# Normalised rows kept in DRAM as two fp16 halves, fp16 products in place of fp32 transposes, and gathers that leave empty places out

## The chip, the cores and the metric

The kernel runs on one core of a Trainium2 chip. The metric is the device time of the whole kernel in microseconds, the median of several executions. TensorE (PE in the profile, with its weight loads as PEld), VectorE (DVE), ScalarE (ACT), GpSimd (POOL) and SyncE (SP, which here only issues transfers) run side by side and meet at semaphores.

## The reference

One pre-norm block on 2 x 1024 tokens of width 512: attention with 32 heads (8 key and value heads of width 16), then a mixture of experts. Only the second half matters here:

```python
flat = x.reshape(b * t, d)                      # 2048 x 512, layer-normalised
logits = flat @ router_w                        # 64 experts
scores = jax.nn.softmax(logits, axis=-1)
_, topk_idx = jax.lax.top_k(logits + router_bias, K)   # K = 4
...
g = jax.nn.silu(jnp.einsum('nd,edf->nef', flat, wg))   # F = 128
u = jnp.einsum('nd,edf->nef', flat, wu)
routed = jnp.einsum('ne,nef,efd->nd', comb, g * u, wd)
...
shared = jnp.einsum('nsh,shd->nd', sg * su, swd)       # 2 shared experts of 512
return (routed + shared).reshape(b, t, d)
```

Each token goes to 4 of 64 experts, so there are 8192 (token, expert) places to compute. With the inputs given, the experts get from 13 to 432 tokens each.

## The kernel before

The attention part is untouched. After it come these stages.

**Normalisation and router.** Tokens stand in 16 tiles of 128, in four groups. TensorE runs, group by group: four output projections (`project`), then for the group before, four transposes of normalised rows (`turn_tokens`, fp32, into PSUM banks 4 and 5 by turns), then their router products (`logits`). `xn2` is a ring of four fp32 tiles of normalised rows, written by VectorE. ScalarE copies each turned tile out of PSUM twice (L900, L901); a bank is free for the next turn only after L901. SyncE stores each normalised tile to `xn2_rows` in DRAM, and after every fourth store issues the load of the next shared weights (`load_stage`). GpSimd is idle until it scales the last shared weights (`swd_scale`, L751).

**Shared experts, routing.** `shared_up` products for the first two groups of 512 tokens. For the first twelve of its 16 chunks `hidden` (L781) is on GpSimd, and TensorE's chunk n waits for `hidden` of chunk n - 2. VectorE works the routing out: places are ordered by expert and cut in tiles of 64, an expert's last tile being partly empty; 192 tiles are laid on 8 lanes of 24 rounds. The table `tab_t` holds for each place its token; an empty place holds 0, so it gathers token 0.

**Routed experts.** 96 pairs of lanes, four to a round, in a loop written out for one round. For pair n GpSimd copies the 128 token numbers (L799) and gathers rows (L801) to the ring `xg` of four tiles. TensorE runs in fixed order: `turn_slots` of pair n + 1 (four fp32 transposes of `xg`, read at every fourth column, L1280), `expert_up` of n (L1293), `turn_hidden` of n - 1 (L1301), `expert_down` of n - 2 (L1309). ScalarE copies the turned rows (L941), VectorE the results (L1668), and ScalarE issues the stores to `slot_y`. SyncE loads an expert's weights to a lane when the lane's expert changes: the up weights of pair n for the next round wait for `e_up` of n in this one, so they have three pairs' time to land. A lane whose expert stays, or that has none, skips its load.

**The rest.** The shared experts of the last two groups of tokens, while GpSimd gathers the rows of `slot_y` and VectorE adds them by gate (`mix`).

In the reference's inputs the 64 experts fill 161 of the 192 tiles; the 12,288 places hold 8192 tokens. Tiles are laid lane by lane, so lane 7 has none, lane 6 none from round 17 on. Counting from the reference's routing, rounds 17, 18 and 19 hold 207, 240 and 189 tokens in 512 places each.

Of the kernel before, what the change touches and what calls it, by code (L numbers as in the profile page):

```python
# [12 lines left out]
P = 128  # L13
# [146 lines left out]
def build_block(nc, x, wq, wk, wv, wo, router_w, router_bias, wgu, wd, swg, swu, swd, out):  # L160
    ctx = ExitStack()
    with ctx:
# [3 lines left out]
        def sem(name):  # L166
            return ctx.enter_context(nc.semaphore(name))
# [25 lines left out]
        k_stacks = nc.dram_tensor("k_stacks", [KVH, 3, HD, NTOK], F16)  # L193
        xn2_rows = nc.dram_tensor("xn2_rows", [NTOK, D], FP32)
        slot_y = nc.dram_tensor("slot_y", [SLOTS, D], FP32)
# [10 lines left out]
        small = sb("small", [P, 1536])  # L206
        ident = sb("ident", [P, P])
        eps_s = sb("eps_s", [P, 1])
        warm = sb("warm", [P, 1])
# [27 lines left out]
        def q_part(u, h, part):  # L237
# [27 lines left out]
        xn2, = carve_all(w_att, 0, ([P, 4, D], FP32))  # L265

        shared_w, swd_w, tmp, mask = carve_all(
            att, 0, ([P, 4, 2 * C * D], F16), ([P, 2, HC * D], F16), ([P, NT, E], FP32),
# [13 lines left out]
        def hidden(n):  # L282
# [10 lines left out]
        lane_w += [carve(flat_xt, n * 3 * C * F, [P, 3, C * F])[0] for n in range(4)]  # L293
        xg, xgt, yb, sg, ht, hg = carve_all(w_att, 0, ([P, 4, D], FP32), ([P, 2, D], FP32), ([P, 2, D], FP32),
                                            ([P, 2, P], FP32), ([P, 2, P], FP32), ([P, 2, P], FP32))
# [22 lines left out]
        ident_zero = sem("ident_zero")  # L318
        ident_set = sem("ident_set")
        mask_zero = sem("mask_zero")  # L320
        mask_steps = sem("mask_steps")
# [50 lines left out]
        xn2_ready = sem("xn2_ready")  # L372
        xn2_stored = sem("xn2_stored")
        turn2_done = sem("turn2_done")
# [86 lines left out]
        def _(sp):  # L461
# [84 lines left out]
            for t in range(NT):  # L546
                sp.wait_ge(xn2_ready, t + 1)
                sp.dma_start(xn2_rows[t * P:(t + 1) * P, :], xn2[:, t % 4, :]).then_inc(xn2_stored, 16)
                if t % 4 == 3:
                    load_stage(2 + t // 4)  # L550
# [50 lines left out]
        def _(pool):  # L601
# [15 lines left out]

            part_scale(0)
            for b in range(BATCH):
                pool.memset(v_head[b][:, :, :], 1 / X_SCALE).then_inc(v_ones, 1)  # L620
# [107 lines left out]
            for l in range(2):  # L728
# [8 lines left out]
                .then_inc(consts, 1)  # L737
            pool.tensor_copy(token_f[:, :], token_f[:, :].bitcast(U32)).then_inc(consts, 1)
            pool.tensor_copy(iota_t[:, :, :], iota_t[:, :, :].bitcast(U32)).then_inc(consts, 1)
            pool.wait_ge(consts, 15)  # L740

            pool.affine_select(out=tile_no[:, LANES:], in_=tile_no[:, LANES:], compare_op=ALU.is_gt, fill=-1.0, base=0,
                               pattern=[[0, LANES]], channel_multiplier=1).then_inc(consts, 1)

            def swd_half(n):
# [49 lines left out]
            def gather_tokens(i, j):  # L795
                n = JP * i + j

                wait(pool, xg_turned, n - 3)
                pool.tensor_copy(idx[:, j:j + 1], tab_t[:, bass.ds(j * LANE_TILES + i, 1)]).then_inc(idx_set, 1)  # L799
                wait_alone(pool, idx_set, n + 1, pool_passed)  # L800
                pool.indirect_dma_start(out=xg[:, j, :], out_offset=None, in_=xn2_rows[:, :],  # L801
                                        in_offset=bass.IndirectOffsetOnAxis(ap=idx[:, j:j + 1], axis=0))\
                    .then_inc(xg_in[j], 16)

            pool.wait_ge(table_ready, 1)
            pool.wait_ge(xn2_stored, 16 * NT)
            for j in range(JP):
# [16 lines left out]
        def _(act):  # L824
# [58 lines left out]
            exps(KVH - 1)  # L883

            for g in range(4):
                act.wait_ge(ln2_aggr, g + 1)
                act.activation(std[:, 4 * g:4 * g + 4], mv[:, 4 * g:4 * g + 4, 1], ACT.Sqrt, bias=eps_s[:, :])\
                   .then_inc(ln2_std, 1)
                act.wait_ge(stage_in[g % 2], 16 * (g // 2 + 1))
                act.activation(shared_w[:, 2 * (g // 2), (g % 2) * C:(g % 2 + 1) * C, :],  # L890
                               w_stage[:, g % 2, :].rearrange("p (c n) -> p c n", c=C), ACT.Copy, scale=W_SCALE)\
                   .then_inc(w_hi_ready, 1)
                for t in range(4 * g, 4 * g + 4):
                    act.wait_ge(turn2_done, t + 1)
                    if t >= 4:

                        act.wait_ge(logits_done, t - 3)
                        act.wait_ge(x_lo_ready, t - 3)
                    src = bank(4 + t % 2).rearrange("p (c t) -> p c t", c=C)
                    act.activation(x_turned[:, t % 4, :, :], src, ACT.Copy).then_inc(xt2_ready, 1)  # L900
                    act.activation(x_hi[:, :, t * P:(t + 1) * P], src, ACT.Copy, scale=X_SCALE).then_inc(x_hi_ready, 1)  # L901
            def swd_high(n):
                act.wait_ge(swd_scaled, n + 1)
                part = slice(n % 2 * C // 2, (n % 2 + 1) * C // 2)
                act.activation(swd_w[:, 0, n * C // 2:(n + 1) * C // 2, :],
                               w_stage[:, n // 2, :].rearrange("p (c n) -> p c n", c=C)[:, part, :], ACT.Copy)\
                   .then_inc(swd_hi_ready, 1)
# [72 lines left out]
        def _(pe):  # L980
# [293 lines left out]
            def turn_slots(n, k, i):  # L1274
                j = k % JP
                pe.wait_ge(xg_in[j], 16 * (i + k // JP + 1))

                wait(pe, xgt_ready, n - 1)
                for c in range(C):
                    mm = pe.transpose(PS[:, (k % 2) * BANK + c * P:(k % 2) * BANK + (c + 1) * P],  # L1280
                                      xg[:, j, c:D:C], ident[:, :])
                mm.then_inc(xg_turned, 1)
# [42 lines left out]

            pe.wait_ge(table_ready, 1)
            turn_slots(0, 0, 0)
            expert_pairs(0, True, False)
# [13 lines left out]
        def _(dve):  # L1342
# [143 lines left out]
            for g in range(4):  # L1486
# [16 lines left out]
                if g:  # L1503

                    dve.wait_ge(xn2_stored, 64 * g)
                    dve.wait_ge(turn2_done, 4 * g)
# [126 lines left out]

            dve.wait_ge(xn2_stored, 16 * NT)
            for k in range(TOPK):
                hot_rows(k)

            for g in range(EARLY):
                for n in range(ON_POOL, HC * (g + 1)) if g else ():
                    shared_hidden(n)  # L1640
                    if n > ON_POOL:
                        hidden_low(n - 1)
                    if n == TABLE_AT + 1:
                        dve.wait_ge(table_done, 1)
                        dve.tensor_copy(tab_t[:, :], bank(6, PAIRS)).then_inc(table_ready, 1)
                if g:
                    hidden_low(HC * (g + 1) - 1)
                for t in range(4 * g, 4 * g + 4) if g else ():
                    shared_add(t)
# [97 lines left out]
```

## Time and profile before

| what | value |
|---|---|
| median of 3 runs | 1257.54 us (1248.75 to 1260.25) |
| the profiled execution | 1258.9 us, its span 1257.2 us |
| mean granted TensorE clock | 0.973 of full speed |
| TensorE busy | 90% of the span |
| VectorE, ScalarE, GpSimd busy | 59%, 40%, 34% |
| HBM read, written | 225.08 MB, 41.42 MB |

Times in the trace are microseconds from the start of the span. The chain of waits is read backwards from the last instruction: each row is what the next one waited for. A matmul's row includes the time until its result is out, so successive starts, not durations, give the pace of TensorE.

### The profile page before, as it was taken

The numbers are of one execution on the slowest core, as the hardware profiler recorded it, in microseconds if no ns is written. First come the engines' busy times: TensorE is split into PE (matmuls) and PEld (weight loads), VectorE is DVE, ScalarE is ACT, GpSimd is POOL, SyncE is SP. The second block draws the span as 40 slices with busy tenths as digits, with TensorE's granted clock in tenths as the row PEclk, the third lists the DMA queues.
The fourth block names the chain that finished last, engine by engine and source line by source line (L and its number), as shares of the span: only waits on it lengthen the run. The fifth ranks groups of instructions, "written<-read, shape, count | busy, mean of one in ns | idle before, by whom it ended". The sixth has DMA issues, their size and how long they took to land.

```text
span 1257.2 us, 27761 instructions
## 1 busy us (share of the span) xinstructions
PE 1136.3 (90%) x9096; PEld 518.4 (41%) x9097; DVE 745.4 (59%) x1198; ACT 501.2 (40%) x944; POOL 423.0 (34%) x548
## 2 busy tenths in 40 slices
PE   6967889988988998998998989999999989997998
PEld 3523233333333332355443445545554444443443
DVE  6746899998999985675798113322333222336373
ACT  3211777887887878434412112222222212211010
POOL 5300233333233333202828322222322222236560
PEclk9978899999999999999999999999999999998999
DMA  8243311221232120242000368878887789656552
GB/s 235 70 132 98 70 45 40 60 55 38 39 74 39 38 51 8 94 142 101 1 1 0 118 210 286 266 251 289 285 266 223 241 281 308 224 132 202 160 168 66
DMA packets 75766, 169.98 MB, mean 135 GB/s; under 512 B 13764, under 2 KB 16324, under 8 KB 75716
## 3 DMA queue, kind: packets, MB, share of 16 engines
q1 hardware_dynamic: 45972, 100.59, 26.6%
q0 software_dynamic: 12800, 41.95, 11.6%
q10 hardware_dynamic: 16944, 26.75, 6.2%
q8 instruction: 34, 0.56, 0.2%
q14 instruction: 16, 0.13, 0.0%
HBM read 225.08 MB, written 41.42 MB: 212 GB/s over the span
## 4 chain that ended last, share of the span: by engine, by line
PE 59%; DVE 18%; issue 9%; DMA 7%; ACT 3%; POOL 1%; SPq 1%; another core or an unknown queue 1%; DVEq 0%; ACTq 0%; POOLq 0%
PE PS L1293 13%; PE PS L1184 9%; PE PS L1309 7%; DVE maxes L1365 7%; PE PS L1101 5%; PE PS L1266 5%; DVE max_low L1367 5%; PE PS L1280 4%; PE PS L989 4%; PE PS L1154 3%; DMA ring<-in_L_ffn_wg_dram 3%; PE PS L1050 2%; PE PS L1079 2%; PE PS L1301 2%; DMA q_stacks<-att 1%
## 5 line engine op out<-in xcount | busy, mean ns | idle before, releaser
L877 ACT ACTIVATE att<-PS 128x512 f32<-128x512 f32 x576 | 312.5, 594 | 93.6 <-PE PS L1079 88.0
L1365 DVE TENSOR_REDUCE maxes<-PS 128x2 f32<-128x128 f32 (+7 forms) x256 | 186.6, 748 | 33.3 <-PE PS L994 33.1
L1184 PE MATMUL PS<-XN,att 128*128 128x512 f16 x768 | 174.6, 389 | 15.6 <-issue 7.7
L1101 PE MATMUL PS<-att,v_head 128*32 128x256 f32 (+1 forms) x2560 | 180.4, 373 | 0.9 <-POOL att L692 0.9
L989 PE MATMUL PS<-att 48*128 48x512 f16 (+7 forms) x768 | 128.3, 332 | 51.1 <-DVE max_low L1367 24.3
L1367 DVE TENSOR_REDUCE max_low<-PS 128x2 f32<-128x1024 f32 x128 | 154.9, 1210 | 11.5 <-PE PS L989 11.0
L1668 DVE COPY w_att<-PS 128x512 f32<-128x512 f32 x96 | 66.4, 692 | 104.1 <-DMA slot_y<-w_att 77.2
L1656 DVE TENSOR_TENSOR w_att<-w_att,PS 128x128 f32<-128x128 f32 x96 | 27.6, 288 | 168.4 <-issue 97.9
L941 ACT ACTIVATE w_att<-PS 128x512 f32<-128x512 f32 x96 | 57.2, 597 | 172.5 <-PE PS L1280 171.6
L692 POOL TENSOR_SCALAR_AFFINE_SELECT att<-att 128x512 f32<-128x512 f32 (+1 forms) x96 | 75.1, 789 | 142.8 <-ACT att L877 141.7
L1184 PEld LDWEIGHTS PS<-XN,att 128*128 128x128 f16 x768 | 76.0, 100 | 112.2 <-issue 19.2
L801 POOL DMA_INDIRECT w_att<-xn_rows,idx x96 | 93.7, 976 | 75.6 <-POOL idx L799 73.2
L1079 PE MATMUL PS<-att 50*128 50x512 f16 (+1 forms) x640 | 113.1, 366 | 5.0 <-ACT att L877 2.6
L989 PEld LDWEIGHTS PS<-att 48*128 48x128 f16 x768 | 37.2, 93 | 185.1 <-DVE maxes L1365 79.9
L1293 PE MATMUL PS<-ring,w_att 128*64 128x256 f32 x768 | 95.0, 390 | 10.5 <-DMA ring<-in_L_ffn_wg_dram 9.4
L1293 PE MATMUL PS<-XT,w_att 128*64 128x256 f32 x768 | 94.6, 389 | 3.3 <-issue 3.3
L919 ACT ACTIVATE w_att<-PS 128x512 f32<-128x512 f32 x32 | 19.1, 597 | 186.5 <-PE PS L1184 136.8
L819 POOL DMA_INDIRECT ring<-slot_y,small x64 | 69.5, 1087 | 68.5 <-DMA slot_y<-w_att 27.5
L1266 PE MATMUL PS<-att,XT 128*128 128x512 f16 x384 | 84.1, 379 | 4.6 <-DVE XT L1621 2.2
L799 POOL COPY idx<-small 128x1 uint32 (+1 forms) x96 | 18.0, 188 | 208.5 <-PE PS L1280 193.5
L1101 PEld LDWEIGHTS PS<-att,v_head 128*32 128x32 f32 x2560 | 56.4, 109 | 72.2 <-issue 45.6
L1280 PEld LDWEIGHTS PS<-ident,w_att 128*128 128x128 f32 x384 | 53.6, 209 | 75.3 <-issue 74.4
(169 smaller groups left out, 1380.2 us busy)
## 6 DMA issues: line engine op xcount, KB each, us to landing
ring<-in_L_ffn_wg_dram SPq DMA_DIRECT2D x96, 512.0 KB
XT<-in_L_ffn_wg_dram SPq DMA_DIRECT2D x96, 512.0 KB
ring<-in_L_ffn_wd_dram SPq DMA_DIRECT2D x96, 256.0 KB
XT<-in_L_ffn_wd_dram SPq DMA_DIRECT2D x96, 256.0 KB
slot_y<-w_att ACTq DMA_DIRECT2D x192, 128.0 KB
att<-q_stacks SPq DMA_DIRECT2D x64, 192.0 KB, 3.8
q_stacks<-att SPq DMA_DIRECT2D x24, 256.0 KB
att<-k_stacks SPq DMA_DIRECT2D x64, 96.0 KB, 3.9
```

The source lines that it names most:

```text
L801: pool.indirect_dma_start(out=xg[:, j, :], out_offset=None, in_=xn2_rows[:, :], in_offset=bass.IndirectOffsetOnAxis(ap=idx[:, j:j + 1], ax ...
L877: act.activation(probs[:, n0 % RING, u * BANK:(u + 1) * BANK], bank((2 * n0 + u) % EXP_BANKS), ACT.Exp, scale=HD ** -0.5 / QK_SCALE ** 2). ...
L989: mm = pe.matmul(bank(at + u, n), q_max[b][rows, t * P:(t + 1) * P], k_max[b][rows, lo:lo + n], start=True, stop=not diagonal)
L1079: mm = pe.matmul(PS[:, at:at + 2 * qn], k_exp[b][rows, kt * P:(kt + 1) * P], q_exp[b][rows, 2 * q0:2 * (q0 + qn)] .rearrange("p (t h q) -> ...
L1101: mm = pe.matmul(PS[32 * r:32 * r + 32, at:at + qn], v_head[b][:, kt, :], probs[:, (NS * b + s) % RING, a:a + qn], start=s in (0, NS0), st ...
L1184: mm = pe.matmul(bank(2 * (n % 2) + k), shared_w[:, 2 * k + w, C * s + c, at:at + P], v[:, c, tokens], start=(c == 0 and w == 0 and v is x ...
L1266: mm = pe.matmul(bank(4 + t % 2), v[:, hc, (t % 4) * P:(t % 4 + 1) * P], swd_w[:, w, hc, :], start=(hc == 0 and w == 0 and v is hidden_hi) ...
L1280: mm = pe.transpose(PS[:, (k % 2) * BANK + c * P:(k % 2) * BANK + (c + 1) * P], xg[:, j, c:D:C], ident[:, :])
L1293: mm = pe.matmul(PS[l * SUB:(l + 1) * SUB, at:at + 2 * F], xgt[:, j % 2, c * P + l * SUB:c * P + (l + 1) * SUB], lane_w[2 * j + l][:, 0:2, ...
L1309: mm = pe.matmul(PS[l * SUB:(l + 1) * SUB, (4 + j % 2) * BANK:(5 + j % 2) * BANK], hg[:, j % 2, l * SUB:(l + 1) * SUB], lane_w[2 * j + l][ ...
L1365: dve.reduce_max(maxes[b][:, :, t], src, AXX).then_inc(side_read, 1)
L1367: dve.reduce_max(max_low[:, :, t - LOW_TILES], src, AXX).then_inc(side_read, 1)
```

## The change

`xn2_rows` gets rows of 1024 fp16 numbers: the high half (the value rounded to fp16, written by ScalarE, `row_high`) and the low half (the rest, by GpSimd, `row_low`), both with the columns reordered so that the four chunks of 128 are contiguous. A row is still 2 KB. `turn_slots` then multiplies both halves by a fp16 identity and sums in PSUM: eight fp16 products instead of four fp32 transposes. Empty places of the table hold 2048 instead of 0, and the gather leaves a number above 2047 out; `xg` is zeroed once first.

```diff
+        row_parts, = carve_all(att, 8192, ([P, 4, 2 * D], F16))
...
             for t in range(NT):
-                sp.wait_ge(xn2_ready, t + 1)
-                sp.dma_start(xn2_rows[t * P:(t + 1) * P, :], xn2[:, t % 4, :]).then_inc(xn2_stored, 16)
+                sp.wait_ge(row_lo_done, t + 1)
+                sp.dma_start(xn2_rows[t * P:(t + 1) * P, :], row_parts[:, t % 4, :])\
+                    .then_inc(xn2_stored[t % 4], 16)
...
+            pool.wait_ge(ident_set, 1)
+            pool.tensor_copy(ident_h[:, :], ident[:, :]).then_inc(ident_h_set, 1)
...
+            def row_low(t):
+                pool.wait_ge(row_hi_done, t + 1)
+                hi, lo = [row_parts[:, t % 4, k * D:(k + 1) * D].rearrange("p (c k) -> p c k", c=C) for k in range(2)]
+                pool.tensor_tensor(lo, xn2[:, t % 4, :].rearrange("p (k c) -> p c k", c=C), hi, ALU.subtract)\
+                    .then_inc(row_lo_done, 1)
+
+            for t in range(NT):
+                row_low(t)
...
                 pool.indirect_dma_start(out=xg[:, j, :], out_offset=None, in_=xn2_rows[:, :],
-                                        in_offset=bass.IndirectOffsetOnAxis(ap=idx[:, j:j + 1], axis=0))\
+                                        in_offset=bass.IndirectOffsetOnAxis(ap=idx[:, j:j + 1], axis=0),
+                                        bounds_check=NTOK - 1, oob_is_err=False)\
                     .then_inc(xg_in[j], 16)
...
+            pool.memset(xg[:, :, :].rearrange("p n d -> p (n d)"), 0.0).then_inc(xg_zero, 1)
+            pool.wait_ge(xg_zero, 1)
...
+            def row_high(g):
+
+                for t in range(4 * g, 4 * g + 4):
+                    act.wait_ge(xn2_ready, t + 1)
+                    if t >= 4:
+                        act.wait_ge(xn2_stored[t % 4], 16 * (t // 4))
+                    act.activation(row_parts[:, t % 4, 0:D].rearrange("p (c k) -> p c k", c=C),
+                                   xn2[:, t % 4, :].rearrange("p (k c) -> p c k", c=C), ACT.Copy).then_inc(row_hi_done, 1)
...
                         act.wait_ge(logits_done, t - 3)
                         act.wait_ge(x_lo_ready, t - 3)
+                    if t % 4 == 0:
+                        row_high(g)
...
                 for c in range(C):
-                    mm = pe.transpose(PS[:, (k % 2) * BANK + c * P:(k % 2) * BANK + (c + 1) * P],
-                                      xg[:, j, c:D:C], ident[:, :])
+                    for part in range(2):
+                        mm = pe.matmul(PS[:, (k % 2) * BANK + c * P:(k % 2) * BANK + (c + 1) * P],
+                                       xg[:, j, part * D + c * P:part * D + (c + 1) * P], ident_h[:, :],
+                                       start=part == 0, stop=part == 1)
...
-                    dve.wait_ge(xn2_stored, 64 * g)
+                    dve.wait_ge(row_lo_done, 4 * g)
                     dve.wait_ge(turn2_done, 4 * g)
...
-                        dve.tensor_copy(tab_t[:, :], bank(6, PAIRS)).then_inc(table_ready, 1)
+                        dve.tensor_scalar(tab_t[:, :], bank(6, PAIRS), float(NTOK), None, ALU.add).then_inc(table_ready, 1)
```

`token_f` holds the token less 2048, which the last line of the diff adds back. `row_parts` lies where the down weights of the shared experts come later, so ScalarE's first `swd_high` waits for all stores.

The order of instructions moves in three places. On ScalarE in the last group of the normalisation stage (PS is PSUM, w_att holds `xn2`, ring the turned fp32 tiles, XN the fp16 ones, att in L915 `row_parts`), before:

```order
L887 ACTIVATE std<-mv,eps_s 128x4 [waits ln2_aggr]
L890 ACTIVATE att<-ring 128x2048 [waits stage_in1]
L900 ACTIVATE ring<-PS 128x512 [waits x_lo_ready,logits_done,turn2_done]
L901 ACTIVATE XN<-PS 128x4x128
...
L919 ACT_TABLE_LOAD
L919 ACTIVATE w_att<-PS 128x512 [waits up_done]
```

and now:

```order
L920 ACTIVATE std<-mv,eps_s 128x4 [waits ln2_aggr]
L923 ACTIVATE att<-ring 128x2048 [waits stage_in1]
L915 ACTIVATE att<-w_att 128x512 [waits xn2_ready,x_lo_ready,xn2_stored0,logits_done,turn2_done]
L915 ACTIVATE att<-w_att 128x512 [waits xn2_stored1,xn2_ready]
L915 ACTIVATE att<-w_att 128x512 [waits xn2_stored2,xn2_ready]
L915 ACTIVATE att<-w_att 128x512 [waits xn2_stored3,xn2_ready]
L935 ACTIVATE ring<-PS 128x512
L936 ACTIVATE XN<-PS 128x4x128
```

The four row copies stand behind the wait for the group's first turn and ahead of the copies that free its banks; so it is in all four groups. On GpSimd, from the last constant of the routing to the first two hidden chunks of the shared experts (ring holds the staged weights), before:

```order
L742 AFFINE_SELECT small<-small 128x8 [waits consts]
L751 TENSOR_SCALAR ring<-ring 128x1024 [waits stage_in0] x2
L781 TENSOR_TENSOR w_att<-w_att 128x512 [waits up_copied,silu_done] x2
L761 TENSOR_TENSOR XT<-w_att,XT 128x512 [waits hidden_hi_done]
L751 TENSOR_SCALAR ring<-ring 128x1024 [waits stage_in1]
```

and now:

```order
L753 AFFINE_SELECT small<-small 128x8 [waits consts]
L759 TENSOR_TENSOR att<-w_att,att 128x512 [waits row_hi_done] x16
L771 TENSOR_SCALAR ring<-ring 128x1024 [waits stage_in0] x2
L801 TENSOR_TENSOR w_att<-w_att 128x512 [waits up_copied,silu_done] x2
L781 TENSOR_TENSOR XT<-w_att,XT 128x512 [waits hidden_hi_done]
```

All sixteen subtractions stand ahead of the scaling of the shared weights, and that ahead of the hidden chunks. On TensorE, one pair of the routed experts in the loop, before:

```order
L1280 MATMUL PS<-ident,w_att 128x128 x4
L1288 REGISTER_ALU
L1293 MATMUL PS<-XT,w_att 64x256 x8
L1301 MATMUL PS<-ident,w_att 128x128
L1309 MATMUL PS<-ring,w_att 64x512 x2
```

and now:

```order
L1319 MATMUL PS<-ident_h,w_att 128x128 x8
L1328 REGISTER_ALU
L1333 MATMUL PS<-XT,w_att 64x256 x8
L1341 MATMUL PS<-ident,w_att 128x128
L1349 MATMUL PS<-ring,w_att 64x512 x2
```

Nothing changes place there; the first row has eight products for four.

## Rows read from the trace of the kernel before

**Rows 1.** The page, busy time by engine, whole span.
```profile
PE 1136.3 (90%) x9096; PEld 518.4 (41%) x9097; DVE 745.4 (59%) x1198; ACT 501.2 (40%) x944; POOL 423.0 (34%) x548
```
**Rows 2.** Stretches: busy time by engine, clock, DMA share and GB/s.
```profile
531.00:596.00 65.00, 59.49 (x363) 37.75 (x361) 43.77 (x76) 26.33 (x44) 6.09 (x3) 1.00 0.37 130
728.00:1115.00 387.00, 371.21 (x2405) 189.94 (x2402) 113.55 (x289) 83.88 (x192) 106.46 (x184) 0.99 0.78 258
```
**Rows 3.** The chain of waits, 580 to 625 us: start, us, what.
```profile
588.86 0.05 ACT ring L900
...
595.43 1.27 POOL w_att L781
...
596.84 22.32 PE PS L1184 x96
```
**Rows 4.** Instructions in order of time, ScalarE, third group's turns.
```profile
571.67 0.60 ACT L900 ACTIVATE ring<-PS 128x512 f32<-128x512 f32 x1 [11.20 <-PE PS L1163]
572.17 0.59 ACT L901 ACTIVATE XN<-PS 128x512 f16<-128x512 f32 x1
```
**Rows 5.** Instructions in order of time, VectorE and GpSimd, 570 to 608 us.
```profile
589.98 0.69 DVE L1480 SCALAR_TENSOR_TENSOR XN<-ring,XN 128x512 f16<-128x512 f32 x1 [7.34 <-ACT XN L901]
...
604.72 3.44 DVE L1545 TENSOR_TENSOR XT<-small 128x1024 bf16<-128x1024 f32 x2
...
570.69 5.52 POOL L751 TENSOR_SCALAR ring<-ring 128x1024 f32<-128x1024 f32 x2 [48.56 <-DMA ring<-in_L_ffn_swd_dram]
...
599.48 1.16 POOL L761 TENSOR_TENSOR XT<-w_att,XT 128x512 f16<-128x512 f32 x1 [1.56 <-ACT XT L911]
...
604.88 2.19 POOL L781 TENSOR_TENSOR w_att<-w_att 128x512 f32<-128x512 f32 x1 [1.51 <-ACT w_att L923]
```
**Rows 6.** Two lines' weight loads: min/median/max ns, first and last start.
```profile
L1163 PEld LDWEIGHTS PS<-ident,w_att x64: 138/140/143, 536.4 to 591.3; 128*128 128x128 f32 x64
...
L1280 PEld LDWEIGHTS PS<-ident,w_att x384: 195/211/220, 728.5 to 1104.2; 128*128 128x128 f32 x192
```
**Rows 7.** Instructions in order of time, TensorE, one pair.
```profile
898.85 0.75 PE L1280 MATMUL PS<-ident,w_att 128*128 128x128 f32 x4
...
902.67 0.75 PE L1280 MATMUL PS<-ident,w_att 128*128 128x128 f32 x4
903.35 1.95 PE L1293 MATMUL PS<-ring,w_att 128*64 128x256 f32 x16
```
**Rows 8.** Instructions in order of time, TensorE, value projections (L1060).
```profile
32.93 2.84 PE L1060 MATMUL PS<-att,XT 128*128 128x128 f16 x48 [0.18 <-POOL att L616]
35.60 5.34 PE L1050 MATMUL PS<-XT,att 128*128 128x512 f16 x24
...
105.71 0.83 PE L1060 MATMUL PS<-att,XT 128*128 128x128 f16 x12
106.48 0.39 PE L989 MATMUL PS<-att 48*128 48x512 f16 x2
```
**Rows 9.** The chain of waits, routed experts: start, us, what.
```profile
742.56 3.15 PE PS L1293 x16
...
1006.74 9.36 DMA ring<-in_L_ffn_wg_dram
...
1042.69 7.93 DMA ring<-in_L_ffn_wg_dram
...
1107.73 1.73 PE PS L1293 x16
```
**Rows 10.** A stretch around one stall, columns as in rows 2.
```profile
1000.00:1020.00 20.00, 16.28 (x100) 8.32 (x96) 4.74 (x13) 3.22 (x7) 4.63 (x8) 0.91 0.88 302
```
**Rows 11.** GpSimd in order of time, then L801 and L645 by line.
```profile
904.56 0.97 POOL L801 DMA_INDIRECT w_att<-xn_rows,idx  x1 [0.79 <-POOL idx L799]
...
L801 POOL DMA_INDIRECT w_att<-xn_rows,idx x96: 970/974/1182, 711.9 to 1090.4; - x96
...
L645 POOL MEMSET att<- x2: 948/948/949, 32.7 to 33.6; 128x1024 f16 x2
```

More of the change, by code:

```diff
@@ L193, in build_block @@
         k_stacks = nc.dram_tensor("k_stacks", [KVH, 3, HD, NTOK], F16)
-        xn2_rows = nc.dram_tensor("xn2_rows", [NTOK, D], FP32)
+        xn2_rows = nc.dram_tensor("xn2_rows", [NTOK, 2 * D], F16)
         slot_y = nc.dram_tensor("slot_y", [SLOTS, D], FP32)
@@ L207, in build_block @@
         ident = sb("ident", [P, P])
+        ident_h = sb("ident_h", [P, P], F16)
         eps_s = sb("eps_s", [P, 1])
@@ L293, in build_block @@
         lane_w += [carve(flat_xt, n * 3 * C * F, [P, 3, C * F])[0] for n in range(4)]
-        xg, xgt, yb, sg, ht, hg = carve_all(w_att, 0, ([P, 4, D], FP32), ([P, 2, D], FP32), ([P, 2, D], FP32),
+        xg, xgt, yb, sg, ht, hg = carve_all(w_att, 0, ([P, 4, 2 * D], F16), ([P, 2, D], FP32), ([P, 2, D], FP32),
                                             ([P, 2, P], FP32), ([P, 2, P], FP32), ([P, 2, P], FP32))
@@ L319, in build_block @@
         ident_set = sem("ident_set")
+        ident_h_set = sem("ident_h_set")
+        row_hi_done = sem("row_hi_done")
+        row_lo_done = sem("row_lo_done")
+        xg_zero = sem("xg_zero")
         mask_zero = sem("mask_zero")
@@ L372, in build_block @@
         xn2_ready = sem("xn2_ready")
-        xn2_stored = sem("xn2_stored")
+        xn2_stored = [sem(f"xn2_stored{n}") for n in range(4)]
         turn2_done = sem("turn2_done")
@@ L737, in _ @@
                 .then_inc(consts, 1)
-            pool.tensor_copy(token_f[:, :], token_f[:, :].bitcast(U32)).then_inc(consts, 1)
+            pool.tensor_scalar(token_f[:, :], token_f[:, :].bitcast(U32), float(-NTOK), None, ALU.add)\
+                .then_inc(consts, 1)
             pool.tensor_copy(iota_t[:, :, :], iota_t[:, :, :].bitcast(U32)).then_inc(consts, 1)
@@ L801, in gather_tokens @@
                 pool.indirect_dma_start(out=xg[:, j, :], out_offset=None, in_=xn2_rows[:, :],
-                                        in_offset=bass.IndirectOffsetOnAxis(ap=idx[:, j:j + 1], axis=0))\
+                                        in_offset=bass.IndirectOffsetOnAxis(ap=idx[:, j:j + 1], axis=0),
+                                        bounds_check=NTOK - 1, oob_is_err=False)\
                     .then_inc(xg_in[j], 16)
             pool.wait_ge(table_ready, 1)
-            pool.wait_ge(xn2_stored, 16 * NT)
+            for n in range(4):
+                pool.wait_ge(xn2_stored[n], 16 * (NT // 4))
+            pool.memset(xg[:, :, :].rearrange("p n d -> p (n d)"), 0.0).then_inc(xg_zero, 1)
+            pool.wait_ge(xg_zero, 1)
             for j in range(JP):
@@ L903, in swd_high @@
                 act.wait_ge(swd_scaled, n + 1)
+                if n == 0:
+                    for m in range(4):
+                        act.wait_ge(xn2_stored[m], 16 * (NT // 4))
                 part = slice(n % 2 * C // 2, (n % 2 + 1) * C // 2)
@@ L1326, in _ @@
             pe.wait_ge(table_ready, 1)
+            pe.wait_ge(ident_h_set, 1)
             turn_slots(0, 0, 0)
@@ L1632, in hot_rows @@
                    .then_inc(tile_hot, 1)
-            dve.wait_ge(xn2_stored, 16 * NT)
+            for n in range(4):
+                dve.wait_ge(xn2_stored[n], 16 * (NT // 4))
             for k in range(TOPK):
```

## The prediction

> **What bounds the kernel now.** I read the busy table first: TensorE 90% [rows 1], so the question is always what moves TensorE. The stretches then give the two stages that the change touches [rows 2]: normalisation and router, 59.5 us of TensorE work in 65 us, and the routed experts, 371.2 in 387, both at full clock. In neither is another engine near its limit; the transfers are at 0.78 in the second. Third, the timeline of one pair of routed experts [rows 7]: turns start at 898.85 and 902.67, so a pair takes 3.82 us, and TensorE's work fills it. Fourth, the chain. In the experts it runs on TensorE and leaves it only where a lane's new weights are late: at 1006.74 a weight transfer holds it for 9.36 us, at 1042.69 another for 7.93 [rows 9]. How much that is in all: from `expert_up` of pair 3 (742.56) to that of pair 95 (1107.73) there are 365.2 us; 92 pairs at 3.825 would be 351.9; 13.3 us are stalls, 3.7 of them in the 20 us around the first of these transfers, where TensorE was busy for 16.28 [rows 10]. Between the stages the chain passes from TensorE to ScalarE at 588.86 (the last group's turned tiles), to GpSimd at 595.43 (`hidden` of chunk 0), and back at 596.84, after which TensorE has work for 22 us without leaving the chain [rows 3]. So in the first stage ScalarE's copies and GpSimd's first chunk are on the path, though both engines are mostly idle.
>
> **The change, part by part**, against the profiled execution (1258.9; the median of the runs is 1.4 lower).
>
> *Row copies on ScalarE, on the path.* In each group TensorE turns two tiles, then waits for ScalarE's L901 to free a bank; ScalarE sat idle 11.2 us before that and starts as soon as the turn is there [rows 4]. Four copies of 128x512 now stand between. Successive copies start 0.50 us apart (571.67, 572.17), so a group gets 1.96 to 2.0 us longer and nothing hides it: the projections behind are in TensorE's order. Four groups: **+7.8 us**. The copies read `xn2` at a step of 16 bytes. The nearest row on such a read is TensorE's own: weight loads of the contiguous `xn2` take 140 ns, of `xg` at the same step 211 [rows 6], half as much again. By that ScalarE's would be 0.73 us, +11.7. I take 7.8, since the 0.50 is ScalarE's own row and the 211 another engine's, and keep 11.7 as the upper end. The lower end is 7: I see no cover for less.
>
> *Row subtractions on GpSimd.* In the first three groups four of them take some 5 us beside ScalarE's copies. VectorE, which now waits for them, waits for the same group's turns anyway, and what it writes then, like the stores and the `load_stage` behind them on SyncE, is wanted a group later, 17.2 us (571.67 to 588.86, [rows 3, 4]): nothing. In the last group, ScalarE starts its copies at 588.86 + 3 x 1.96 = 594.7, GpSimd its first subtraction at 595.3. A like operation (L761, two inputs, fp16 out) takes 1.16 us alone [rows 5]; four end at 600.0. VectorE's four L1480 (0.69 each) fall in there, and GpSimd operations that meet VectorE's with two inputs get longer (L781 from 1.27 to 2.19 beside L1545): I add 1.5, so 601.5. Behind them stand two `swd_scale`, which before had been done at 570.69, where GpSimd was idle (5.52 for two, so 607.0), then `hidden` of chunk 0 (1.27 and 0.14 to TensorE): 608.4, where it was 596.84. That is 11.6 in all, 3.8 beyond ScalarE's 7.8. If the 16-byte step costs GpSimd the half that it costs the weight loads, four times 0.58 come on top: 6.1. Between these I take the middle, **+5.0**; ends 3 and 9. Late next would be the routing's `ranks` on TensorE; VectorE is delayed only by ScalarE's part and has slack against TensorE there, so the whole delay is passed on. `load_stage` of the last weights is issued only after the last subtraction, near 603, and is wanted by the third `swd_scale` near 611; 1 MB at the 302 GB/s of [rows 10] is 3.5 us, an estimate, so it is in time.
>
> On the lock behind these longer operations the Trainium skill (SBUF — State Buffer, "SBUF: two separate sides") says that a VectorE operation with two SBUF inputs and a GpSimd one that reads SBUF exclude each other for a whole instruction. The 2.19 agrees. By that rule all four L1480 would be waited for in full, 2.8 instead of my 1.5, and the sum would be 1.3 higher.
>
> *Small things.* The fp16 identity is one GpSimd copy while it waits for weights; `token_f` and `tab_t` are exchanged one for one. Zeroing `xg` (4096 fp16) is four times L645's 0.95 = 3.8 us; the first gather was issued at 711.9 and the first turn came at 728.5 [rows 6, 11], so 17 us of shared experts cover it; without that cover it would cost 3.8. **0.**
>
> *Turning the slots.* Before, 0.68 us from the first turn to the first `expert_up` [rows 7]. The value projections are the same products (128x128 fp16 weights, 128 columns): 48 in 2.67 us, 0.0556 each; and twelve of them before another kind took 0.77, which is 12 x 0.0556 and 0.10 for the changeover [rows 8]. Eight then take 0.445 + 0.10 = 0.545, a gain of 0.135 a pair, over 95 pairs **-12.8 us**. Ends: with no changeover 0.235 (-22); with a second changeover 0.035 (-3).
>
> *Gathers.* 4096 of 12,288 places are empty: 8.4 MB less. That is worth only what it takes off the stalls. In the stretch around the largest one the core moved 302 GB/s at a share of 0.88 [rows 10]; a round's four gathers are 1.05 MB in 15.3 us. In rounds 17 to 19 between 47% and 37% of the places are filled, so some 0.6 MB go, 2.1 us at that rate. At the two late transfers of [rows 9] I take 2.1 each, at the other places, with fuller rounds, 1.5 in all. Against it, weights have three pairs' time to land, and that gets 3 x 0.135 = 0.4 shorter, at five stalls 2.0. Together -3.7, of which I take **-3.0**; ends +2 (no relief) and -9.
>
> *Sum.* 7.8 + 5.0 - 12.8 - 3.0 = **-3.0**: 1255.9 by the profiled execution, 1254.5 by the median; I say **1255**. A measurement of this kernel can tell a difference of about 1% (12.6 us) from none.
>
> **The rivals.**
>
> *A. The strided reads cost more (ends slower than before).* ScalarE at 0.73: copies of the last group start at 597.5, the first subtraction at 598.3; four at 1.74 and 1.5 of meetings end at 606.8; `swd_scale` 612.3; TensorE resumes at 613.7, 16.9 us late. With the rule of whole operations and longer `swd_scale` beside VectorE's search, 20. Gains stay 15.8. +1 to +4: **1261**. It decides when the first stage's delay passes 15.8 us. For it: the 211 against 140 ns. Against: no row shows ScalarE or GpSimd slowed by a step.
> The Trainium skill (GPSIMD Engine Reference, "Performance pitfalls for Q7 kernels") prices SBUF reads at steps above 8 bytes at half as much again. It would make GpSimd's part 6.1 rather than 3.8. No row here shows GpSimd at such a step.
>
> *B. GpSimd's gather becomes the bound.* A gather with a limit may take longer to issue. Gap and gather are 0.79 + 0.97 = 1.76 us of a pair's 3.69 [rows 11], with the short copy of the numbers under 2. It decides from a gather of 2.7 us; at 2.9, 95 pairs would lose 0.2 each: +19 - 3, **1273**. Nothing speaks for it.
>
> *C. Everything gained.* The changeover is hidden, -22, and the stalls mostly go, -9; the cost is 12.8: -18, **1239**. For it: the weight stalls lie where the gathers are emptiest.
>
> *D. Leaving out doesn't relieve.* Skipped places cost the queues what they cost before, or the stalls are a matter of when the weights are issued: +2 instead of -3: **1260**.
>
> **How the numbers follow.** Forecast 0.50 (1250 to 1260), A 0.17, B 0.06, C 0.15, D 0.12. All but B and C lie within 1%. Taking the bounds at both ends, the range is **1240 to 1269**. Faster by over 1% is C and a little of the forecast's lower side, 0.19; slower is B and the upper end of A, 0.12; within 1%, 0.69.
>
> **What would show it.** ScalarE: sixteen copies of 0.6 us, four before each group's first L900's like, and groups of 19.1 us instead of 17.2. GpSimd: subtractions of 1.2 us or, if A, 1.7; TensorE's gap before its third shared chunk 10 to 13 us longer in place. A pair at 3.69 us in place of 3.825. Stalls from pair 3 to 95 near 10 us. If TensorE's pair is not shorter, the turning term is wrong; if the stage ahead of the experts is longer by over 16 us, A.

## The result: 1.3% slower, where the forecast was 0.2% faster

| | before | changed |
|---|---|---|
| median | 1258.34 us (4 runs) | 1274.53 us (4 runs) |
| ratio, 95% interval | 1 | 1.0127 (1.0091 to 1.0163) |
| span of the profiled execution | 1257.2 us | 1271.0 us |
| mean granted TensorE clock | 0.973 | 0.958 |

One execution of a later run, the repeated early copies, took 2635.21 us, for a reason that is not known, and is left out of that run's median and ratio.

The chain of waits of the changed kernel, at the first `expert_up`, at that of pair 3 and at the last one (start, us, what):

```profile
762.09 1.95 PE PS L1333 x16
...
772.83 1.95 PE PS L1333 x16
...
1117.47 1.73 PE PS L1333 x16
```

The first `expert_up` starts at 762.09, 31.9 us later than before (730.17); from it to the last one there are 355.4 us instead of 377.6; the end is 13.8 us later. So the stage ahead lost 32, the experts gave 22.2 back, and 4.1 went in the tail, which no part of the change touches. The experts' gain is larger than forecast (15.8). The loss ahead of them is two and a half times the 12.8 that were forecast, and all of it lies in the normalisation stage. The stretches say what kind of loss it is (columns as in [rows 2]; 531 to 630 answers to the first of them, the next two are in it):

```profile
531.00:630.00 99.00, 79.45 (x355) 54.07 (x352) 42.90 (x72) 43.11 (x60) 29.27 (x19) 0.75 0.25 85
...
541.00:549.00 8.00, 8.00 (x40) 7.75 (x38) 4.92 (x10) 4.50 (x7) 1.02 (x1) 0.50 0.59 199
...
555.00:561.00 6.00, 6.00 (x29) 2.71 (x28) 1.38 (x2) 0.00 (x0) 0.00 (x0) 1.00 0.00 0
```

TensorE's work, nearly the same instructions, is 79.5 us instead of 59.5, at a granted clock of 0.75; inside a group the clock is 0.50, which is its level of 1.2 GHz, and back at 1.00 some 14 us later. TensorE and ScalarE in order of time show where it falls, in the first group:

```profile
534.75 1.04 PE L1201 MATMUL PS<-ident,w_att 128*128 128x128 f32 x8
540.64 2.05 PE L1201 MATMUL PS<-ident,w_att 128*128 128x128 f32 x8 [4.86 <-ACT XN L936]
542.49 6.93 PE L1209 MATMUL PS<-router_s,ring 128*128 128x64 f32 x32
549.21 12.17 PE L1192 MATMUL PS<-att,XT 128*128 128x512 f16 x48
561.22 1.04 PE L1201 MATMUL PS<-ident,w_att 128*128 128x128 f32 x8
```
```profile
535.38 4.15 ACT L915 ACTIVATE att<-w_att 128x512 f16<-128x512 f32 x4 [5.05 <-PE PS L1201]
...
588.74 4.15 ACT L915 ACTIVATE att<-w_att 128x512 f16<-128x512 f32 x4 [16.47 <-PE PS L1201]
```

ScalarE's four copies take 4.15 us, 1.03 each. TensorE sits idle for 4.86 us after two turns, and after that everything is slow: eight turns in 2.05 us, 32 router products in 6.93 (before: 3.68), and part of the projections. A group is 26.5 us (534.75 to 561.22; the next two take 26.9 and 27.1), where ScalarE's turned copies were 17.2 us apart [rows 3, 4].

One pair of routed experts in the changed kernel, which answers to [rows 7]:

```profile
902.99 0.62 PE L1319 MATMUL PS<-ident_h,w_att 128*128 128x128 f16 x8
903.54 1.95 PE L1333 MATMUL PS<-XT,w_att 128*64 128x256 f32 x16
905.41 0.33 PE L1341 MATMUL PS<-ident,w_att 128*128 128x128 f32 x1
905.67 1.08 PE L1349 MATMUL PS<-ring,w_att 128*64 128x512 f32 x4
906.69 0.62 PE L1319 MATMUL PS<-ident_h,w_att 128*128 128x128 f16 x8
```

The turn takes 0.55 us (902.99 to 903.54), a pair 3.70. From pair 3 (772.83) to pair 95 there are 344.6 us; 92 pairs at 3.70 are 340.4, so 4.2 us of stalls are left of 13.3.

### The profile page after: what moved, and what is told of

Its sections match the earlier page's. It is cut to its first block, busy times and chain, and to the rows that moved or that the text cites. A ratio compares the mean times of both kernels' runs of the same rounds, so it can differ in the third digit from the quotient of the medians.

```text
span 1271.0 us, 28676 instructions
## 1 busy us (share of the span) xinstructions
PE 1142.1 (90%) x9480; PEld 523.4 (41%) x9481; DVE 750.1 (59%) x1198; ACT 517.5 (41%) x960; POOL 453.7 (36%) x566
## 4 chain that ended last, share of the span: by engine, by line
PE 64%; DVE 17%; issue 8%; DMA 4%; ACT 3%; POOL 1%; SPq 1%; DVEq 0%; ACTq 0%; POOLq 0%
PE PS L1333 14%; PE PS L1222 10%; PE PS L1349 7%; DVE maxes L1406 7%; PE PS L1304 6%; PE PS L1139 5%; DVE max_low L1408 4%; PE PS L1319 4%; PE PS L1027 4%; PE PS L1192 4%; PE PS L1088 2%; PE PS L1117 2%; PE PS L1341 2%; PE PS L1209 2%; DMA q_stacks<-att 1%
## 5 line engine op out<-in xcount | busy, mean ns | idle before, releaser
L1222 PE MATMUL PS<-XN,att 128*128 128x512 f16 x768 | 178.3, 394 | 16.0 <-issue 7.8
L1408 DVE TENSOR_REDUCE max_low<-PS 128x2 f32<-128x1024 f32 x128 | 154.8, 1210 | 11.9 <-PE PS L1027 11.7
L821 POOL DMA_INDIRECT w_att<-xn_rows,idx x96 | 99.1, 1032 | 81.8 <-POOL idx L819 78.3
L1222 PEld LDWEIGHTS PS<-XN,att 128*128 128x128 f16 x768 | 76.6, 101 | 115.8 <-issue 22.7
L984 ACT ACTIVATE w_att<-PS 128x128 f32<-128x128 f32 x96 | 26.6, 277 | 132.3 <-PE PS L1333 102.5
L1319 PEld LDWEIGHTS PS<-ident_h,w_att 128*128 128x128 f16 x768 | 43.3, 98 | 75.3 <-issue 75.0
```

What stands on the lines that cost most here:

```text
L1222: mm = pe.matmul(bank(2 * (n % 2) + k), shared_w[:, 2 * k + w, C * s + c, at:at + P], v[:, c, tokens], start=(c == 0 and w == 0 and v is x ...
L1319: mm = pe.matmul(PS[:, (k % 2) * BANK + c * P:(k % 2) * BANK + (c + 1) * P], xg[:, j, part * D + c * P:part * D + (c + 1) * P], ident_h[:, :],
L1408: dve.reduce_max(max_low[:, :, t - LOW_TILES], src, AXX).then_inc(side_read, 1)
```

## The experiments

All ratios are against the kernel before, run beside on the same chip, with the 95% interval.

**Theory 1**: ScalarE's copies, where they stand, open a gap on TensorE in each group, and TensorE comes back from it at half clock; the clock costs more than the gap. **Theory 2**: the stage is slow because of the added work itself, GpSimd's subtractions and the loads behind them, or reads beside TensorE's.

### The copies early

```diff
             for g in range(4):
                 ...
+                row_high(g)
                 for t in range(4 * g, 4 * g + 4):
                     act.wait_ge(turn2_done, t + 1)
                     ...
-                    if t % 4 == 0:
-                        row_high(g)
```

Expected:

> The changed kernel with one edit: ScalarE's four row copies of a group stand ahead of its wait for the group's first turn, where ScalarE is idle for 11 us (5 us in the first group), instead of behind it. Theory 1 (the copies open a gap of 4.9 us on TensorE in each group, and TensorE comes back from it at half clock): both go, the normalisation stage takes 65 us again instead of 99, granted clock 1.00 there, the kernel 1258 - 22 = 1236 us (1231 to 1242). Theory 2 (the stage is slower because GpSimd's sixteen subtractions and the later load of the shared down weights stand in the way, or because ScalarE's and GpSimd's reads disturb TensorE's): the work is the same, the stage stays above 85 us, the kernel above 1258.

Measured: 1233.99 us against 1251.83, ratio 0.9846 (0.9803 to 0.9888); once more on another chip:

> The kernel with the early copies once more, on the same chip as the spread places, for a comparison free of the chip. It should repeat its ratio of 0.985 (0.981 to 0.989), with 4 to 6 us of stalls.

Measured: 1239.13 against 1259.94, ratio 0.9835 (0.9796 to 0.9873); the stalls from pair 3 on are 4.1 us in the first of these runs and 5.4 in the second. From the first run, the stretch that answers to the first of [rows 2], TensorE's gap and GpSimd:

```profile
531.00:596.00 65.00, 60.27 (x362) 37.40 (x360) 45.46 (x82) 41.32 (x57) 39.87 (x18) 1.00 0.37 130
```
```profile
558.05 0.63 PE L1200 MATMUL PS<-ident,w_att 128*128 128x128 f32 x4 [0.83 <-ACT XN L935]
559.03 0.63 PE L1200 MATMUL PS<-ident,w_att 128*128 128x128 f32 x4 [0.35 <-ACT XN L935]
559.50 3.68 PE L1208 MATMUL PS<-router_s,ring 128*128 128x64 f32 x32
```
```profile
581.10 9.15 POOL L759 TENSOR_TENSOR att<-w_att,att 128x512 f16<-128x512 f32 x4 [7.99 <-ACT att L915]
590.23 5.51 POOL L771 TENSOR_SCALAR ring<-ring 128x1024 f32<-128x1024 f32 x2
597.77 2.49 POOL L801 TENSOR_TENSOR w_att<-w_att 128x512 f32<-128x512 f32 x2 [2.04 <-ACT w_att L960]
```

The same copies and subtractions cost nothing here: clock 1.00, gap 0.83 us, a group 17.2. The last group's four subtractions even take 9.15 us, where those of the changed kernel take 5.4 to 5.9 a group (the first of them stand beside VectorE's L1520 and L1554, 580.28 to 584.98), and are still done before GpSimd is wanted. Theory 2 falls. This version beats both kernels.

### TensorE kept busy through the gap

```diff
             def turn_tokens(t):
                 ...
+                if t % 4 == 1:
+                    for n in range(20):
+                        pe.matmul(bank(4 + t % 2), wo_hi[:, n % C, 0:P], wo_lo[:, n % C, :], start=True, stop=True)
                 for c in range(C):
                     mm = pe.transpose(...)
```

and, in the second run, 40 transposes of the tile to the same bank in their place:

```diff
+                    for n in range(40):
+                        pe.transpose(PS[:, (4 + t % 2) * BANK + n % C * P:(4 + t % 2) * BANK + (n % C + 1) * P],
+                                     xn2[:, t % 4, n % C * P:(n % C + 1) * P], ident[:, :])
```

Expected:

> The changed kernel, and TensorE computes 20 fp16 products of 512 columns (some 4.3 us) into the free bank between the first and the second turn of each group; their result is written over. They add work and take no wait away. Theory 1: TensorE is busy through ScalarE's copies, the clock stays at 1.00 from the second group on, router products take 3.7 us a group instead of 6.9 and the projections behind them 10.5 instead of 12.2, a group 22 us instead of 26.9: the kernel 1253 to 1258 us, 17 to 21 below the changed one. Theory 2 (the products are slow for another reason, reads beside ScalarE's): no gain, 1274 or some us more.

> As the run with filling products, but the filler is 40 more fp32 transposes of the group's second tile (some 4.5 us at 0.11 us each), written over as well. If transposes keep the clock up as products do: 1253 to 1259 us, clock 1.00 in the stage. If a transpose counts as no work for the clock: the clock falls as in the changed kernel, each transpose takes twice as long, 1274 to 1285 us.

Measured: 1250.28 and 1250.41 against 1251.83, ratios 0.9993 (0.9967 to 1.0018) and 0.9983 (0.9951 to 1.0014). Added work makes the changed kernel 1.3% faster. With the filling transposes:

```profile
560.13 0.60 PE L1205 MATMUL PS<-ident,w_att 128*128 128x128 f32 x4
560.57 4.53 PE L1202 MATMUL PS<-ident,w_att 128*128 128x128 f32 x40
564.93 0.60 PE L1205 MATMUL PS<-ident,w_att 128*128 128x128 f32 x4
566.21 0.63 PE L1205 MATMUL PS<-ident,w_att 128*128 128x128 f32 x4 [0.68 <-ACT XN L936]
```

and with the filling products:

```profile
558.58 0.63 PE L1204 MATMUL PS<-ident,w_att 128*128 128x128 f32 x4 [0.62 <-ACT XN L936]
559.55 0.63 PE L1204 MATMUL PS<-ident,w_att 128*128 128x128 f32 x4 [0.34 <-ACT XN L936]
560.02 3.68 PE L1212 MATMUL PS<-router_s,ring 128*128 128x64 f32 x32
```

ScalarE holds the banks as long as in the changed kernel, but router products are at 3.68 us. A group takes 21.3 to 21.4 us. So the wait for the banks costs about 4.1 us a group, and the clock 5 to 6 more. Here GpSimd does come into the way: with TensorE at full pace it waits 4.03 us for the first hidden chunk, 2.4 more than before (1.62), which is the term forecast at 5.0; in the changed kernel TensorE was so late that 0.36 was left of it.

The Trainium skill (TensorE: Matmul & The Clock Gate, "Part 4: PE-mode transpose") says that a transpose doesn't count as work for the clock as a product does. Here the measurement differs: with 40 fp32 transposes in the gap (4.53 us) the granted clock stayed at 1.00 behind it in all four groups, as with 20 fp16 products (4.48 us).

### The step of the read

```diff
-    act.activation(row_parts[:, t % 4, 0:D].rearrange("p (c k) -> p c k", c=C),
-                   xn2[:, t % 4, :].rearrange("p (k c) -> p c k", c=C), ACT.Copy).then_inc(row_hi_done, 1)
+    act.activation(row_parts[:, t % 4, 0:D], xn2[:, t % 4, :], ACT.Copy).then_inc(row_hi_done, 1)
...
-    xg[:, j, part * D + c * P:part * D + (c + 1) * P]
+    xg[:, j, part * D + c:(part + 1) * D:C]
```

and the subtraction likewise. Expected:

> The changed kernel, but the halves keep the columns in their order: ScalarE and GpSimd read the fp32 rows contiguously, and TensorE reads the gathered halves at every fourth column instead (a step of 8 bytes). If the step of 16 bytes is what doubles ScalarE's copy: 0.50 us each instead of 1.03, the gap on TensorE 2.7 us instead of 4.9, GpSimd 1.16 instead of 1.36. By theory 1 the shorter gap costs at least 2.1 us less a group, 1266 at most; if it is also short enough for the clock to hold, 1250 or less (a group 19.2 us). Weight loads of the slots at a step of 8 bytes may take longer than 98 ns; if the pace of a pair stays 3.70 us they are hidden.

Measured: 1257.84 against 1251.83, ratio 1.0058 (1.0022 to 1.0094). In order of time, ScalarE, then TensorE:

```profile
558.39 2.19 ACT L915 ACTIVATE att<-w_att 128x512 f16<-128x512 f32 x4 [15.45 <-PE PS L1200]
```
```profile
561.70 0.72 PE L1200 MATMUL PS<-ident,w_att 128*128 128x128 f32 x4 [2.90 <-ACT XN L935]
562.67 1.08 PE L1200 MATMUL PS<-ident,w_att 128*128 128x128 f32 x4 [0.26 <-ACT XN L935]
563.55 6.92 PE L1208 MATMUL PS<-router_s,ring 128*128 128x64 f32 x32
```
```profile
559.10 4.50 POOL L759 TENSOR_TENSOR att<-w_att,att 128x512 f16<-128x512 f32 x4 [19.40 <-ACT att L915]
```

The step of 16 bytes is what doubled ScalarE's copies: 2.19 us for four at a step of 4 bytes, 4.15 at 16. GpSimd's four subtractions take 4.50 us instead of 5.4. And without the step the clock falls too, after a gap of 2.90 us: this is exactly the 2 us a group that the prediction had priced, and router products behind it still run at half clock. Read at a step of 8 bytes the slots' weight loads take 113 ns instead of 98; a pair takes 3.72 us for 3.70, so nearly all of that is hidden.

### How long a gap

To see this away from the change, the kernel before got two idle copies on ScalarE:

```diff
                 for t in range(4 * g, 4 * g + 4):
                     act.wait_ge(turn2_done, t + 1)
+                    if t % 4 == 0:
+                        for n in range(2):
+                            act.activation(spare[:, n, :], xn2[:, 0, :], ACT.Copy)
```

Expected:

> The kernel before, with two more copies of 128x512 on ScalarE (contiguous, to a spare place, read by nobody) ahead of each group's turned copies. They lengthen TensorE's gap in each group from 0.83 to 1.8 us and do nothing else. Known: a gap of 0.83 us leaves the clock at 1.00, one of 2.9 us (plain columns) brings the slow stretch. If the clock also falls after 1.8 us: a group 22 us or more instead of 17.2, the kernel 18 us or more slower, ratio 1.014 or more. If it holds: a group 18.2 us, 4 us slower, ratio 1.003.

Measured: 1271.83 against 1260.73, ratio 1.0107 (1.005 to 1.0163), between the two expectations:

```profile
536.75 0.63 PE L1167 MATMUL PS<-ident,w_att 128*128 128x128 f32 x4 [1.86 <-ACT XN L905]
537.73 0.63 PE L1167 MATMUL PS<-ident,w_att 128*128 128x128 f32 x4 [0.35 <-ACT XN L905]
538.19 6.68 PE L1175 MATMUL PS<-router_s,ring 128*128 128x64 f32 x32
...
559.93 0.63 PE L1167 MATMUL PS<-ident,w_att 128*128 128x128 f32 x4 [1.86 <-ACT XN L905]
560.90 0.63 PE L1167 MATMUL PS<-ident,w_att 128*128 128x128 f32 x4 [0.35 <-ACT XN L905]
561.37 3.68 PE L1175 MATMUL PS<-router_s,ring 128*128 128x64 f32 x32
```

The same gap of 1.86 us was followed by the low clock in the first group and not in the second; the third and the fourth had it again. One microsecond of waiting more costs 1 us in one group (18.2 us, 557.03 to 575.25) and 6 in another (23.2 us, 533.85 to 557.03).

The length of the gap doesn't decide it alone. The kernel before has the low clock too, where its stage ends (TensorE alone; columns: stretch, us, busy, clock, DMA share, GB/s) and behind the stall of [rows 10]:

```profile
596.00:600.00 4.00, 3.16 (x8) 0.57 0.00 0
600.00:604.00 4.00, 4.00 (x20) 1.00 0.00 0
...
1016.00:1020.00 4.00, 3.58 (x17) 0.57 1.04 413
1020.00:1024.00 4.00, 4.00 (x28) 1.00 0.88 290
```

The first comes after a wait of 1.62 us (for GpSimd's chunk 0), the second after one of 3.72. In the changed kernel, against that, a wait of 2.93 us left the clock at 1.00:

```profile
721.48 4.71 PE L1222 MATMUL PS<-XN,att 128*128 128x512 f16 x21 [2.93 <-POOL w_att L801]
```
```profile
718.00:722.00 4.00, 1.07 (x6) 1.00 0.00 0
722.00:726.00 4.00, 4.00 (x20) 1.00 0.02 4
```

Behind the gaps inside the groups the clock stayed low for 10 to 14 us, behind these two for some 4. What makes the difference was not tried.

### What leaving places out is worth

Two runs take the other half of the change apart: the early copies with every place gathered again,

```diff
-            pool.tensor_scalar(token_f[:, :], token_f[:, :].bitcast(U32), float(-NTOK), None, ALU.add)\
+            pool.tensor_copy(token_f[:, :], token_f[:, :].bitcast(U32))\
                 .then_inc(consts, 1)
...
-                                        bounds_check=NTOK - 1, oob_is_err=False)\
...
-    dve.tensor_scalar(tab_t[:, :], bank(6, PAIRS), float(NTOK), None, ALU.add).then_inc(table_ready, 1)
+    dve.tensor_copy(tab_t[:, :], bank(6, PAIRS)).then_inc(table_ready, 1)
```

and the kernel before with the reverse of this edit and the zeroing of `xg`. Expected:

> The kernel of the run with the early copies, but every place is gathered again, an empty one token 0 (no limit on the gather, the table as before the change). So of the change only the fp16 halves and the products are left, without the wait. A pair should stay at 3.70 us, 11.9 us off 95 pairs. Theory A (leaving places out is what shrank the weight stalls from 13.3 to some 5 us): the stalls come back and more, 13 to 16 us, since weights have 0.4 us less to land; the kernel 8 to 10 us above the early copies' ratio of 0.985, so 0.991 to 0.993 of before. Theory B (the stalls shrank for another reason, such as where the shorter pair puts the loads): stalls near 5 us, ratio 0.984 to 0.987.

> The kernel before with one part of the change alone: empty places left out of the gathers (and the ring of gathered rows zeroed once); rows stay fp32, turned by fp32 transposes. Theory A: a pair stays at 3.825 us and the stalls from pair 3 on fall from 13.3 us to 3 to 6: 7 to 10 us gained, ratio 0.992 to 0.994. Theory B: no change, ratio 0.998 to 1.002. A gather takes GpSimd 1.03 instead of 0.98 us, which is hidden.

Measured: all places 1255.23 against 1260.73, ratio 0.995 (0.9926 to 0.9974); leaving out alone 1248.67, ratio 0.9913 (0.9881 to 0.9946). The first and the last `expert_up` of the reckoning, with all places, then with leaving out alone:

```profile
742.99 3.50 PE PS L1330 x16
...
1105.85 1.73 PE PS L1330 x16
```
```profile
737.69 1.95 PE PS L1298 x16
...
1091.21 1.73 PE PS L1298 x16
```

With all places and pairs of 3.70, 362.9 us hold 22.5 of stalls; with leaving out alone and pairs of 3.825, 353.5 hold 1.6. Theory A stands, and its size was underrated. By these traces leaving out is worth 11.7 us (13.3 to 1.6) in the kernel before and 18.3 behind the shorter pair (22.5 to 4.2). One trace each is rough, though. The kernel before with idle copies, whose routed part is that of the kernel before, has 8.3 us of stalls where that one had 13.3:

```profile
753.05 3.28 PE PS L1297 x16
...
1113.28 1.73 PE PS L1297 x16
```

Part of the stalls is the clock again: an `expert_up` like this one, or like the 3.50 us above, stands behind a wait and is slow itself, which makes its pair 1.6 us longer. With all places five pairs are so, in the kernel before two, with places left out none or one. And the traced execution with all places was 6.0 us slower than its median. By ratios (0.995 against 0.9835 and 0.9846) leaving out behind the shorter pair is worth 13 to 14 us, and alone in the kernel before 11 (0.9913).

The bytes saved are 8.4 of the 99.8 MB moved from 730 to 1115 us, which seems little for that. Before, all empty places gathered the same row:

```diff
+    dve.scalar_tensor_tensor(out=spread[:, 1, :], in0=bank(6, PAIRS), scalar=0.0, in1=spread[:, 0, :],
+                             op0=ALU.is_equal, op1=ALU.mult).then_inc(spread_in, 1)
+    dve.wait_ge(spread_in, 1)
+    dve.scalar_tensor_tensor(out=tab_t[:, :], in0=bank(6, PAIRS), scalar=float(NTOK),
+                             in1=spread[:, 1, :], op0=ALU.add, op1=ALU.add).then_inc(table_ready, 1)
```

(`spread[:, 0]` holds 16q - 2048 in row q, and the gather has no limit.) Expected:

> The early copies, every place gathered, but an empty place of row q gathers token 16q instead of token 0 (worked out in the table), so that no two empty places of a gather read the same row. Bytes are as in the run with all places. Theory A1 (leaving out pays by the bytes and packets it saves): stalls as with all places, 15 to 21 us, ratio 0.993 to 0.997. Theory A2 (it pays because the empty places all read one row of DRAM, which is slow): most stalls gone, 5 to 10 us left, ratio 0.985 to 0.988.

Measured: 1244.29 against 1259.94, ratio 0.9893 (0.9856 to 0.993), beside 0.9835 of the early copies on the same chip. Its `expert_up` of pair 3 and of pair 95:

```profile
732.34 1.95 PE PS L1339 x16
...
1083.49 1.73 PE PS L1339 x16
```

351.2 us hold 10.8 of stalls, between the 22.5 with all places on one row and the 4.2 to 5.4 with places left out. Neither A1 nor A2 alone: both not reading one row again and again and reading less seem to count. The traces give 11.7 us to the first and 6.6 to the second, but the execution traced here was 7.2 us faster than its median; by the ratios (0.995, 0.9893, 0.9835) each is worth about 7 us. The intervals of neighbours touch or overlap, so neither half is clear of noise by itself; the two together are. How one row delays the weights is open. The gathers' own packets hardly show it: from 745 to 1090 us 22.80 MB of them took 22.7% of the DMA engines' time with one row, and 22.29 MB took 21.0% with spread rows.

## Why the prediction was wrong

- **Row copies on ScalarE: +7.8, "a group gets 1.96 to 2.0 us longer and nothing hides it".** This is the step that failed, twice. The copy took 1.03 us, not 0.49: the upper end (0.73) was short of it, since I had only another engine's row on such a read, and none of ScalarE's. And the price of the wait was taken as its length. The stage's term missing from the sum is TensorE's clock: behind a gap of 4.86 us (and, with plain columns, of 2.90) it ran at half pace for 10 to 14 us. Against the forecast of +7.8 the third shared chunk came 33.4 us later (630.20 for 596.84): about 16 by the longer gaps of the four groups and about 20 by the clock, less the 1.3 that TensorE no longer waits for GpSimd and the 1.9 by which the stage had begun earlier. I had taken full clock from the means of [rows 2], and passed over the sign in [rows 10], a granted clock of 0.91 around a stall: there TensorE lost not the 3.7 us that I read off but 5.4, the wait of 3.72 and 1.6 more for an `expert_up` at low clock (3.51 us for 1.95):

  ```profile
  1016.42 3.51 PE L1293 MATMUL PS<-ring,w_att 128*64 128x256 f32 x16 [3.72 <-DMA ring<-in_L_ffn_wg_dram]
  ```

  So the price of a longer gap was not zero by the rows that I had; it should have been bounded by what the stage takes at half clock.
- **Subtractions on GpSimd: +5.0.** The mechanism was there but hidden: 2.4 us with TensorE kept at pace, 0.4 in the changed kernel. A subtraction took 1.36 us (5.44 for four), between my 1.16 and 1.74, and about a fifth more than with plain columns (4.50 for four), not a half. Meeting VectorE's four L1480 (now L1521) cost little: the last group's four took 5.88 us and the two scalings behind them 5.95 for 5.52, together 0.9 more, where I had 1.5 and the rule of whole operations 2.8.
- **Turning the slots: -12.8.** Right: 0.55 us forecast and measured, a pair 3.70 for 3.69, 11.9 us over 95 pairs.
- **Gathers: -3.0.** Right in sign, too small: stalls fell from 13.3 to 4.2, by 9.1, the end of the bounds. With the shorter pair working against it, leaving out was worth 13 to 18 us. I had priced bytes; the repeated row and the clock behind the longer stalls were not in the price.
- **Small things: 0.** Held: the stretch from the third shared chunk to the first `expert_up` was 133.3 us before (596.84 to 730.17) and 131.9 after.
- The rivals: A had the right sign and the right first cause, but ended at 1261, because it too priced a wait at its length. The range of 1240 to 1269 was also narrower than its own ends: 11.7 + 9 - 3 + 2 is 19.7 above the kernel before, 1277. A range up to there would have held the 1274.5, but by luck, since none of these ends contains the clock. That the change as such is good and its place bad was none of my cases.

The sum with what was measured: 33 in the stage, -1.4 behind it, -22.2 in the experts, +4 in the tail give the 13.8 us by which the spans differ. The 4 us of the tail are not explained; the time from the last `expert_up` to the end lies between 147.3 and 153.6 us in all eleven traces, though no edit touches it, and no experiment was made on it.

## What to carry to other kernels

Ask of each added wait on TensorE not only how long it is but what clock stands behind gaps of that length elsewhere in the trace, in short stretches, since a mean over a stage hides it. Where it falls behind some of them, or the trace has none so long, give the work behind the wait at half pace as the upper end of its price. A step that needs only what has long been ready goes ahead of the wait for what is late (moving one call up by a few lines was worth 2.8%, 1.0127 against 0.9846). Padding indices are best left out; where they can't be, spreading them over many rows probably helps, by about 7 us here.

## What the runs showed of the hardware

- TensorE's clock: it held behind gaps of 0.83 us (before) and 0.62 to 0.68 (filled) and fell behind 2.90 and 4.86 in all four groups. Between them it went either way: it fell behind 1.86 in three groups of four and behind 1.62 at the end of the stage, and held behind 2.93 later in the changed kernel.
- ScalarE's copy of 128x512 fp32 to fp16 from SBUF: 0.55 us read contiguously, 1.03 at a step of 16 bytes. GpSimd's subtraction: 1.36 at that step, 1.13 without it.
- The Trainium skill (SBUF — State Buffer, "Door 1: The DMA port swizzle (why `[64,N]` ≈ `[32,N]`)") has lines of 16 bytes in SBUF and a penalty for an access that leaves its line; ScalarE's doubled copy agrees, at 1.03 us instead of 0.55.
- A gather that leaves places out takes GpSimd 1.03 us to issue instead of 0.98, whether they are many or few in this kernel.
